# Heads and output weights split into a rounded part and a rest, with the orders of four engines laid anew, in an attention block with a feed-forward part

## The reference

```python
x = x + layernorm(attn(layernorm(x), Wqkv, Wo))
x = x + layernorm(tanh(layernorm(x) @ W1 @ W2 @ W3 + bias))

def attn(x, Wqkv, Wo):                       # per batch element, T = 256, H = 8, D = 64
    q, k, v = split(einsum('bte,fe->btf', x, Wqkv).reshape(B, T, H, 3 * D), 3)
    q, k = q + pe, k + pe                    # a table of sines and cosines
    scores = where(causal, q @ k.T / sqrt(D), -inf)
    heads = softmax(scores) @ v              # 256 x 512 over all heads
    return einsum('btf,ef->bte', heads, Wo)  # the heads' sum: 512 -> 128
```

## Time and profile before

| | us |
|---|---|
| median of 3 runs | 573.59 (572.29 to 573.95) |
| the profiled execution | 574.77 |
| its span, first to last instruction | 573.0 |
| PE busy | 535.5 (93% of the span) |
| weight loads on PE (beside the products) | 456.3 (80%) |
| DVE busy | 467.6 (82%) |
| ACT busy | 409.0 (71%) |
| POOL busy | 407.5 (71%) |

### The profile page before, as it was taken

The page is one execution under the profiler, slowest core; times in us unless marked ns, Lnnn a source line. Parts: engine busy times, 40 slices in busy tenths (PEclk is TensorE's granted clock), DMA queues, the critical chain, the costliest instruction groups (busy, mean ns, idle before and its releaser), DMA issues.

```text
span 573.0 us, 16766 instructions
## 1 busy us (share of the span) xinstructions
PE 535.5 (93%) x4580; PEld 456.3 (80%) x4580; DVE 467.6 (82%) x2053; ACT 409.0 (71%) x1505; POOL 407.5 (71%) x659
## 2 busy tenths in 40 slices
PE   1799999999999999999999999999999999999961
PEld 0578888888888888888888888888888888888740
DVE  3488888889888888888888889888888898888721
ACT  0277787777777877787778777877777778778730
POOL 4236578777787787777877777777777777875656
PEclk9999999999999999999999999999999999999985
DMA  4100001000000000000100001000000000000000
GB/s 137 37 11 19 11 20 29 25 15 27 27 27 23 22 27 15 22 27 27 27 18 27 27 9 27 27 27 27 18 27 27 10 27 27 27 18 11 20 9 18
DMA packets 27674, 14.53 MB, mean 25 GB/s; under 512 B 1667, under 2 KB 27398, under 8 KB 27654
## 3 DMA queue, kind: packets, MB, share of 16 engines
q1 hardware_dynamic: 26694, 12.85, 8.0%
q10 hardware_dynamic: 960, 1.44, 0.7%
HBM read 10.09 MB, written 4.19 MB: 25 GB/s over the span
## 4 chain that ended last, share of the span: by engine, by line
PE 91%; ACT 2%; POOL 2%; issue 1%; DVE 1%; DMA 1%; SPq 1%; POOLq 0%; DVEq 0%; ACTq 0%
PE scores L671 17%; PE turned_and_heads L722 16%; PE misc_bank L775 11%; PE qk_bank L686 6%; PE qk_bank L688 5%; PE qk_bank L687 5%; PE turned_probs L699 5%; PE turned_probs L700 5%; PE turned_and_heads L708 5%; PE misc_bank L657 4%; PE misc_bank L760 3%; PE misc_bank L659 3%; PE misc_bank L658 3%; PE misc_bank L728 2%; PE misc_bank L758 1%
## 5 line engine op out<-in xcount | busy, mean ns | idle before, releaser
L247 ACT ACTIVATE probs<-scores,neg_max 128x256 f32<-128x256 f32 (+1 forms) x512 | 209.1, 427 | 40.9 <-DVE neg_max L545 40.8
L545 DVE CUSTOM_DVE_ANT_0 scores<-scores,mask 128x256 f32<-128x256 f32 (+1 forms) x512 | 166.4, 387 | 11.3 <-PE scores L671 11.2
L555 DVE TENSOR_TENSOR qk<-qk_bank,pe 128x512 f32<-128x512 f32 x128 | 87.5, 684 | 33.1 <-PE qk_bank L688 26.0
L392 POOL TENSOR_TENSOR probs<-probs,inv_sum 128x512 f32<-128x512 f32 (+1 forms) x128 | 103.1, 825 | 16.0 <-DVE inv_sum L561 16.0
L671 PE MATMUL scores<-qk 64*128 64x256 f32 (+1 forms) x1024 | 107.8, 344 | 1.3 <-DVE qk L555 0.6
L247 ACT ACTIVATION_READ_ACCUMULATOR probs<-scores,neg_max 128x1 f32 x512 | 108.0, 211 | 0.0
L671 PEld LDWEIGHTS scores<-qk 64*128 64x128 f32 x1024 | 88.7, 188 | 18.9 <-issue 11.7
L722 PE MATMUL turned_and_heads<-pt,vals 128*64 128x256 f32 (+1 forms) x1024 | 98.1, 334 | 2.4 <-ACT pt L267 2.4
L722 PEld LDWEIGHTS turned_and_heads<-pt,vals 128*64 128x64 f32 x1024 | 64.1, 137 | 28.7 <-issue 2.8
L686 PE MATMUL qk_bank<-xt_hi,w_hi 128*128 128x256 f32 x256 | 81.0, 316 | 1.1 <-DVE xt_lo L593 0.9
L265 ACT COPY pt<-turned_probs 128x512 f32<-128x512 f32 x128 | 76.5, 598 | 7.8 <-PE turned_probs L700 4.1
(11 more groups left out here) (80 smaller groups left out, 1013.6 us busy)
## 6 DMA issues: line engine op xcount, KB each, us to landing
x_in<-in_x SPq DMA_DIRECT2D x32, 128.0 KB, 2.2
x_res<-in_x SPq DMA_DIRECT2D x32, 128.0 KB, 2.1
out_x<-x SPq DMA_DIRECT2D x32, 128.0 KB, 1.8
w_raw<-in_w_qkv_t ACTq DMA_DIRECT2D x1, 768.0 KB, 4.7
pe<-pe_table ACTq DMA_DIRECT2D x1, 256.0 KB, 4.7
wo<-in_w_o_t ACTq DMA_DIRECT2D x1, 256.0 KB, 5.8
mask<-causal_mask ACTq DMA_DIRECT2D x1, 128.0 KB, 5.3
w_sb<-in_w SPq DMA_DIRECT2D x2, 64.0 KB, 5.5
```

The lines of the kernel that those rows point to most:

```text
L247: ins = nc.scalar.activation(probs[k][j][:, h, lo:hi], s_bank[j][:, h, lo:hi], ACT.Exp, bias=neg_max[k][j][:, i:i + 1], scale=-1.0, accum_ ...
L392: ins = nc.gpsimd.tensor_tensor(some, some, inv, ALU.mult)
L545: ins = nc.vector.tensor_tensor_reduce(some, some, mask[:, t * P:2 * P], -1.0, HIGHEST, ALU.add, ALU.min, neg_max[k][j][:, i:i + 1])
L555: nc.vector.tensor_tensor(qk[j][:, :], qk_bank[:, :], pe[:, :], ALU.add).then_inc(qk_kept, 1)
```

## The change

Output weights and heads are each kept as a float32r part and a float32r rest, and the heads' sum is made of three float32r products in place of each plain one, so 24 in place of 8 per element. The rounded copies of both halves of the heads are ACT's, the rests are DVE's. The slot lists of ACT, POOL, DVE and PE are in a new order; the steps in them are otherwise the same. SP's list is not touched.

```diff
--- before.py
+++ after.py
@@ -97,6 +97,7 @@
         wo = sb("wo", [P, PAIRS, E])
+        wo_hi, wo_lo = sb("wo_hi", [P, PAIRS, E], F32R), sb("wo_lo", [P, PAIRS, E], F32R)
...
@@ -116,7 +117,7 @@
-        heads_t = two("heads_t", [P, PAIRS, T])
+        heads_hi, heads_lo = two("heads_hi", [P, PAIRS, T], F32R), two("heads_lo", [P, PAIRS, T], F32R)
...
@@ -267,15 +269,15 @@
                 nc.scalar.copy(pt1[j][:, :, :], heads_bank[:, 0:2 * P].rearrange("p (h t) -> p h t", h=2)
                                ).then_inc(pt1_kept, 1)
 
-            def keep_heads(b):
-
-                if not b.exists():
-                    return
-                act.wait_ge(heads_made, units(b, 2))
+            def keep_heads(b, k):
+
+                if not b.exists():
+                    return
+                act.wait_ge(heads_made, units(b, k + 1))
 
                 wait(act, attn_made, b.times(1, -1))
-                nc.scalar.copy(heads_t[b.parity][:, 2:4, :], heads_bank[:, :].rearrange("p (j t) -> p j t", j=2)
-                               ).then_inc(heads_kept[1], 1)
+                nc.scalar.copy(heads_hi[b.parity][:, 2 * k:2 * k + 2, :], heads_bank[:, :].rearrange("p (j t) -> p j t", j=2)
+                               ).then_inc(heads_hi_kept, 1)
 
             def keep_x_hi(b):
                 if not b.exists():
@@ -315,22 +317,23 @@
 
             def slot(b, k):
                 if k == 0:
-                    keep_turned(b.plus(-1), 0, 1)
-                    keep_vals(b, 0)
-                    exps(b, 0, 0)
                     keep_vals(b, 1)
-                    keep_turned(b.plus(-1), 1, 0)
                     exps(b, 0, 1)
-                    keep_turned(b.plus(-1), 1, 1)
                     keep_x_hi(b.plus(1))
                     keep_y(b.plus(-2))
+                    keep_heads(b.plus(-1), 1)
+                    tanh(b.plus(-2))
                 else:
-                    keep_heads(b.plus(-1))
-                    tanh(b.plus(-2))
+                    keep_turned(b, 0, 0)
                     exps(b, 1, 0)
+                    keep_turned(b, 0, 1)
                     keep_attn(b.plus(-1))
-                    keep_turned(b, 0, 0)
                     exps(b, 1, 1)
+                    keep_heads(b, 0)
+                    keep_turned(b, 1, 0)
+                    keep_vals(b.plus(1), 0)
+                    keep_turned(b, 1, 1)
+                    exps(b.plus(1), 0, 0)
 
             all_slots(act, slot)
 
@@ -444,15 +447,15 @@
 
             def slot(b, k):
                 if k == 0:
-                    rstd_attn(b.plus(-2))
-                    make_x1(b.plus(-2))
-                    scale_probs(b.plus(-1), 1)
-                    norm_y(b.plus(-2))
                     norm_ffn(b.plus(-3))
+                    scale_probs(b, 0)
                 else:
-                    scale_probs(b, 0)
                     make_out(b.plus(-3))
                     norm_x(b.plus(2))
+                    rstd_attn(b.plus(-1))
+                    scale_probs(b, 1)
+                    make_x1(b.plus(-1))
+                    norm_y(b.plus(-1))
 
             all_slots(pool, slot)
 
@@ -466,6 +469,11 @@
                 nc.vector.tensor_copy(w_hi[:, :], w_raw[:, :]).then_inc(ready_split, 1)
                 dve.wait_ge(ready_split, 2)
                 nc.vector.tensor_tensor(w_lo[:, :], w_raw[:, :], w_hi[:, :].bitcast(F32), ALU.subtract
+                                        ).then_inc(ready_split, 1)
+
+                nc.vector.tensor_copy(wo_hi[:, :, :], wo[:, :, :]).then_inc(ready_split, 1)
+                dve.wait_ge(ready_split, 4)
+                nc.vector.tensor_tensor(wo_lo[:, :, :], wo[:, :, :], wo_hi[:, :, :].bitcast(F32), ALU.subtract
                                         ).then_inc(ready_split, 1)
 
                 dve.wait_ge(fused_pe, 1)
@@ -571,15 +579,15 @@
                     ins = nc.vector.tensor_tensor(some, some, inv, ALU.mult)
                 ins.then_inc(scaled[0], 1)
 
-            def keep_heads(b):
-
-                if not b.exists():
-                    return
-                dve.wait_ge(heads_made, units(b, 1))
+            def keep_heads_rest(b, k):
+                if not b.exists():
+                    return
+                dve.wait_ge(heads_hi_kept, units(b, k + 1))
 
                 wait(dve, attn_made, b.times(1, -1))
-                nc.vector.tensor_copy(heads_t[b.parity][:, 0:2, :], heads_bank[:, :].rearrange("p (j t) -> p j t", j=2)
-                                      ).then_inc(heads_kept[0], 1)
+                h = slice(2 * k, 2 * k + 2)
+                nc.vector.tensor_tensor(heads_lo[b.parity][:, h, :], heads_bank[:, :].rearrange("p (j t) -> p j t", j=2),
+                                        heads_hi[b.parity][:, h, :].bitcast(F32), ALU.subtract).then_inc(heads_kept[k], 1)
 
             def keep_x_lo(b):
                 if not b.exists():
@@ -595,35 +603,36 @@
 
             def slot(b, k):
                 if k == 0:
+                    invert_sums(b.plus(-1), 1, 1)
+                    stats_ffn(b.plus(-3))
+                    keep_heads_rest(b.plus(-1), 0)
                     norm_attn(b.plus(-2))
-                    invert_sums(b.plus(-1), 1, 1)
                     row_max(b, 0, 0)
                     stats_y(b.plus(-2))
                     nc.vector.drain()
                     take_moments("y", b.plus(-2))
-                    keep_heads(b.plus(-1))
+                    row_max(b, 0, 1)
                     keep_qk(b, 1, 0)
-                    row_max(b, 0, 1)
-                    stats_ffn(b.plus(-3))
+                    stats_x(b.plus(2))
                     wait_stats("ffn", b.plus(-3))
                     invert_sums(b, 0, 0)
                     take_moments("ffn", b.plus(-3))
+                    scale_probs(b, 0)
+                    wait_stats("x", b.plus(2))
                     keep_qk(b, 1, 1)
-                    stats_x(b.plus(2))
-                    scale_probs(b, 0)
+                    take_moments("x", b.plus(2))
                     invert_sums(b, 0, 1)
+                    keep_x_lo(b.plus(1))
                 else:
-                    keep_x_lo(b.plus(1))
+                    keep_heads_rest(b.plus(-1), 1)
                     row_max(b, 1, 0)
-                    wait_stats("x", b.plus(2))
+                    row_max(b, 1, 1)
                     keep_qk(b.plus(1), 0, 0)
-                    take_moments("x", b.plus(2))
-                    row_max(b, 1, 1)
+                    invert_sums(b, 1, 0)
+                    scale_probs(b, 1)
                     stats_attn(b.plus(-1))
-                    wait_stats("attn", b.plus(-1))
-                    invert_sums(b, 1, 0)
+                    nc.vector.drain()
                     take_moments("attn", b.plus(-1))
-                    scale_probs(b, 1)
                     keep_qk(b.plus(1), 0, 1)
 
             all_slots(dve, slot, prepare)
@@ -636,7 +645,7 @@
             mm(misc_bank[:, 0:P], w2_sb[:, :], w1t_sb[:, :], start=True, stop=True).then_inc(fused_pe, 1)
             pe_eng.wait_ge(fused_dve, 1)
             mm(misc_bank[:, P:2 * P], w12t_sb[:, :], w3_sb[:, :], start=True, stop=True).then_inc(fused_pe, 1)
-            pe_eng.wait_ge(ready_split, 3)
+            pe_eng.wait_ge(ready_split, 5)
             pe_eng.wait_ge(fused_dve, 2)
             pe_eng.wait_ge(bias_ready, 3)
 
@@ -772,33 +781,36 @@
                     if b.plus(2).exists():
                         pe_eng.wait_ge(x_lo_kept, b.times(1, 3))
                 for p in range(PAIRS):
-                    ins = mm(misc_bank[:, t * E:(t + 1) * E], heads_t[b.parity][:, p, t * P:(t + 1) * P], wo[:, p, :],
-                             start=(p == 0), stop=(p == PAIRS - 1))
+                    hi, lo = heads_hi[b.parity][:, p, t * P:(t + 1) * P], heads_lo[b.parity][:, p, t * P:(t + 1) * P]
+                    to = misc_bank[:, t * E:(t + 1) * E]
+                    mm(to, hi, wo_hi[:, p, :], start=(p == 0), stop=False)
+                    mm(to, hi, wo_lo[:, p, :], start=False, stop=False)
+                    ins = mm(to, lo, wo_hi[:, p, :], start=False, stop=(p == PAIRS - 1))
                 if t == 1:
                     ins.then_inc(attn_made, 1)
 
             def slot(b, k):
                 if k == 0:
+                    make_vals(b, 0)
+                    turn_probs(b.plus(-1), 1, 1)
                     make_qk(b, 1, 0)
                     make_vals(b, 1)
-                    turn_probs(b.plus(-1), 1, 0)
+                    make_heads(b.plus(-1), 1)
                     make_qk(b, 1, 1)
-                else:
                     turn_x(b.plus(1))
-                    turn_probs(b.plus(-1), 1, 1)
                     turn_y(b.plus(-2))
                     make_scores(b, 1)
-                    make_heads(b.plus(-1), 1)
+                else:
                     make_ffn(b.plus(-2))
+                    turn_probs(b, 0, 0)
```

(10 more changed lines are left out.)

## The result

The changed kernel takes 595.65 us (median of 4, 594.72 to 596.54) against 573.77 for the kernel before on the same chip: a ratio of 1.0384, 95% interval 1.0355 to 1.0412. It is slower, by 21.9 us; 597 was forecast.

The account below looks back on a forecast made before the run. PE's queue was taken as the bound, busy for all 16.47 us of a period. Products +0.78 and order -0.05 give +0.73 per element, 32 times +23.4, so 597 us from a median of 573.59, range 581 to 613.

Parts of the forecast that it names:

- (1): Heads' sum on PE: 24 one-pass records at 0.110 replace 16 at 0.116, +0.78 us per element.
- (2): Added heads copies on ACT (+0.59) and rests on DVE (+0.69): covered, taken as nothing, up to 0.2 kept.
- the cover: Room on ACT and DVE in a period over 17 us, hiding added copies; without it up to 0.69 per element.
- (3): New slot lists: waits removed against entries and near-waits added, -0.05 us per element, ends -0.3 and +0.3.
- The waits of the old order: PE's waits at heads' sum, value product and scores: 0.14 + 0.24 + 0.17 = 0.55 us a period, all to go.
- The new costs: In the new order: 0.3 for scores and heads standing apart, plus 0.1 and 0.1 for two new waits.
- The two near-waits: PE ahead of turn_probs(b-1, 1, 1), 0.1 short, and ahead of make_ffn, a tie taken as 0.1.
- The run of ACT before make_ffn: Copies and exponentials, then DVE's rest and PE's lead: 6.04 us against PE's own 5.99, a tie.
- (4): One-time split of the output weights, two DVE passes bounded by 0.69 each, while PE waits anyway; taken as 0.
- A (columns decide): Rival for the heads' sum: load hidden, 0.060 a product, -0.47 per element, 558.5 us; chance 0.13.
- B (a plain product's price, 0.231): Rival: narrow rounded products in the heads' sum cost as plain ones, +3.65 per element, 690 us; chance 0.10.
- C (ACT's run as the bound): Rival: make_ffn comes 0.3 to 0.6 later each time, +1.2 per element, 613 to 616 us; chance 0.07.

Follow-up runs that it names:

- e4: Changed kernel with all copies and rests made, but the heads' sum as eight plain fp32 products of the rounded heads by whole weights; 569.49 us.
- e9: Kernel before, old lists and its two heads copies (now rounding), with 24 one-pass products and no rests made; 601.94 us.
- e3: Changed kernel with each of the 24 products done as two of 64 moving columns; 691.25 us.
- e6: Changed kernel with each of the 24 products given only 64 of its 128 weight columns; 567.87 us.
- e1: Changed kernel's new lists with the old heads' sum: eight plain products, single copies, no split; 568.71 us.
- e2: Kernel before, old lists, with the new heads' sum: 24 products, rounded copies by ACT, rests by DVE; 622.69 us.
- e10: Old lists with rounded copies and rests (k = 0 by DVE alone), but eight plain products, rests left out of the sum; 596.51 us.

## Why the prediction was right

(1) *Three products for each plain one.* Taken as +0.78 a period with a price of 0.110. The price is 0.111, and the step is +0.83 in the new order (e4 to the changed kernel) and +0.86 in the old (e9). The mechanism is the weight load: e3 and e6 show it from both sides. The small miss is in the plain products, for which I took 1.86 from a place where I thought that nothing held them. It was held: the last copy of the heads ended there at 46.02 + 0.59 = 46.61, 0.11 before the first product, as the timeline of the kernel before shows.

```profile
46.02 0.59 ACT L277 COPY heads_t<-turned_and_heads 128x512 f32<-128x512 f32 x1 [1.54 <-PE turned_and_heads L722]
...
46.72 2.01 PE L775 MATMUL misc_bank<-wo,heads_t 128*128 128x128 f32 x16
```

Free, the sum is 2 x 0.89 = 1.78 (e1). So PE wants what it waits for 0.49 us ahead and not 0.42 (295.26 - 1.78 - 292.99), and the value product gives 0.49 too. That a rounded product is one record where a plain one is two was true and beside the point, since each record has its load: per element 16 loads became 24.

Of the Trainium skill's fast load for operands that are not fp32 ("TensorE: Matmul & The Clock Gate", Weight-path perf modes) no trace here shows anything for rounded operands: 194 ns and a price of 0.111. The same page of the Trainium skill (LDWEIGHTS) has P / 1.2 ns for a load of P columns, by which I estimate 107 ns and 53 ns for 128 and 64 columns; 0.111 in the changed kernel agrees with the first, and the 0.06 of e6 lies just over the second, where 128 moving columns bound it as well.

(2) *Copies.* Taken as 0, and 0 in the new order (e4 against e1). That this hung on the order I had bounded by 0.69 if the cover were gone; the same copies in the old order cost 0.65 (e2 less e9). That the two are so near is partly chance: the bound is one pass of DVE, and e10, with two added passes on DVE, has 0.67 as well.

(3) *The order.* Taken as -0.05, measured as -0.21 (e1). The waits of the old order did go, and they were 0.62 and not 0.55, since the sum is 1.78 when it is free (1.99 - 1.78 = 0.21). The new costs were less than the 0.5 I set against them: the heads cost 1.45 also apart from the scores, so only leaving the scores is new, 0.26 - 0.11 = 0.15. The two near-waits came, each in one of two periods only: ahead of make_ffn 0.10 (0.04 + 0.28 for 0.22) and ahead of the second turn of probabilities 0.09 (0.20 for 0.11), where I took 0.1 each for every period. (The run of ACT before make_ffn adds up to 6.06 and not 6.04, which changes nothing.)

One cost I had not seen. In the other of the two periods the value product takes 0.45 for 0.23, and no engine holds it: the timeline of weight loads puts the gap down to issue.

```profile
294.92 0.19 PEld L666 LDWEIGHTS misc_bank<-w_hi,xt_hi 128*128 128x128 f32 x1 [0.19 <-issue]
```

This product is the first step of PE's new list, and the loop runs two elements per pass. Over the whole trace it starts 0.23 to 0.26 after the record before it at 12 places, every second period from 124 to 500 us, and 0.03 after it at all others, those of the unrolled ends among them. The loop over 26 elements has 12 such returns. So it is the return of the loop, 0.22 in one of two periods. In the old list the step behind that return was a projection behind the heads' products, which costs 0.32 in every period, at the return or not. No run moved the return to another step.

Together: -0.62 + 0.15 + (0.22 + 0.10 + 0.09) / 2 = -0.265, and with 24 x 0.111 - 1.78 = +0.884 for the products +0.62, where +0.63 was measured.

(4) *Once.* Taken as 0, measured as 2.9 us before the first copy. The same is in e1 (2.8) and e4 (2.5), so it comes with the order and not with the split. The chain of waits between 17 and 36 us after has exponentials and copies of ACT in a row where the pipeline is still filling; which step of the new lists it is was not taken apart.

The sum: +0.73 a period was forecast and +0.63 came. In the 31 steps between first and last copy that is 18.4 us where 22.6 was forecast, 4.2 less, and a 32nd step that I counted (0.7) isn't there; the ramp gave 2.9 back. The misses had opposite signs, so that the total is within 2 us of the forecast is in part luck, and the total is nearer than its terms.

The rivals: A (columns decide) falls with the price of 0.111, and e6 shows the 0.06 that it had counted on, for half the weights. B (a plain product's price, 0.231) falls with it too. C (ACT's run as the bound) had the right place, the wait ahead of make_ffn, and a tenth of its size: 0.10 in one of two periods for 0.3 to 0.6 in each.

## What to carry to other kernels

Count weight loads before passes: with 128 weight columns and 128 moving ones, a plain fp32 product of two records and a rounded one cost 0.22 and 0.11, so three rounded ones for one plain one is 1.5 times the time. With 256 moving columns the split should pay, by an estimate: three rounded ones at 0.12 are 0.36, a plain one is two records of 0.22 by the prediction's figure, 0.44; no run here tried it. When a change has two parts, run each alone: here one part was a gain of 0.21 us a period and the other a loss of 0.83, four times as large. Copies that are free in one order cost 0.65 us a period in another, and busy shares do not tell which: DVE is busy for 31.3 of 32.5 us in e4 (290 to 322.5), where they are free, and for 29.4 of 35.9 in e2 (290 to 325.9), where they are not. When lists are laid anew, look also at which step stands first in the loop: its return costs time where nothing else hides it.

## What the runs showed of the hardware that was not expected

In e3, PE had products without a gap and its granted clock fell all the same. Late in the run, in every second period, after two stretches of 24 products of 64 moving columns each (566.7 to 572.5), the granted clock is 0.73 and 0.70 in the two windows of 3 us behind them, a mean of full speed and the lower of the two levels (1.2 GHz). Read us by us from 573 to 577 it is 0.69, 0.50, 0.50 and 0.60, and 1.00 on either side. In its busy time by window the columns are as in the earlier trace rows:

```profile
569.00:572.00 3.00, 3.00 (x30) 3.00 (x29) 1.03 (x2) 0.86 (x2) 0.74 (x1) 1.00 0.13 31
572.00:575.00 3.00, 3.00 (x22) 2.36 (x23) 1.69 (x7) 2.00 (x9) 0.96 (x3) 0.73 0.00 0
575.00:578.00 3.00, 3.00 (x25) 2.16 (x22) 1.50 (x6) 0.59 (x1) 1.54 (x2) 0.70 0.00 0
578.00:581.00 3.00, 3.00 (x23) 2.66 (x24) 2.86 (x18) 2.34 (x6) 1.54 (x3) 1.00 0.15 44
```

The heads behind them take 2.73 in its chain in place of 1.45, and such a period 21.2 in place of 19.75. The same two stretches stand in every period of e3, and up to the 21st copy none is followed by such a period, so what sets the fall off stays open. In the changed kernel, with 128 moving columns and half as many products, the periods stay at 17.1 to the end of the loop and the clock stays full.

```profile
573.38 2.73 PE turned_and_heads L731 x16
```
